# Loading a transformer block's weights behind three semaphores, with the first queries finished beside the first keys

## What is computed

```
x = x + xattn(layernorm(x), ctx)       # q = xn @ Wq + bq; k, v = ctx @ Wk + bk, ctx @ Wv + bv; rope on q and k
x = x + gla(layernorm(x))              # Wq, Wk, Wg1, Wg2, Wv, Wg of its own, scan over 64 tokens, Wo
x = x + ffn(layernorm(x))              # shared expert + 2 of 7 routed experts, hidden width 704
```

## Time and profile before

| | |
|---|---|
| median of 3 runs | 2244.09 us (2237.24 to 2244.69) |
| the profiled execution's own time | 2234.34 us |
| its span in the trace | 2232.5 us |
| busy PE / DVE / ACT / POOL | 1782.9 / 1487.8 / 1097.5 / 748.8 us |
| share of the chain that ended last | PE 43%, DVE 16%, issue 6%, ACT 4%, POOL 3% |

### The profile page before, as it was taken

One profiled execution on the slowest core, in us unless ns is written; L12 is line 12 of the kernel. 1 busy time (PEld: TensorE's weight loads), 2 busy tenths in 40 slices (PEclk: granted clock), 3 DMA queues, 4 the chain that ended last, 5 costly groups with the idle time before them and its releaser, 6 DMA issues.

```text
span 2232.5 us, 51528 instructions
## 1 busy us (share of the span) xinstructions
PE 1782.9 (80%) x19596; PEld 1321.3 (59%) x19596; DVE 1487.8 (67%) x2914; ACT 1097.5 (49%) x2670; POOL 748.8 (34%) x850
## 2 busy tenths in 40 slices
PE   2787787778777877787778777657688999999997
PEld 1454555555555555555555555435567888888886
DVE  1787777877877788788777887746554444444447
ACT  1556555655555556555655565533353333333332
POOL 2333243333333333334333434214501333333320
PEclk8888888989889888888898988868899999999999
DMA  3200010001000100010000000003241111111143
GB/s 84 67 17 17 17 32 17 17 17 32 17 17 17 32 17 17 17 32 17 17 20 29 17 17 19 4 3 107 76 130 43 49 47 44 46 49 46 42 155 125
DMA packets 64092, 88.35 MB, mean 40 GB/s; under 512 B 9488, under 2 KB 52128, under 8 KB 63856
## 3 DMA queue, kind: packets, MB, share of 16 engines
q1 hardware_dynamic: 41232, 36.29, 5.4%
q0 software_dynamic: 10752, 33.17, 4.2%
q10 hardware_dynamic: 11872, 15.60, 2.2%
HBM read 66.68 MB, written 18.35 MB: 38 GB/s over the span
## 4 chain that ended last, share of the span: by engine, by line
PE 43%; DVE 16%; issue 6%; ACT 4%; POOL 3%; ACTq 1%; DMA 0%; DVEq 0%; SPq 0%; POOLq 0%
PE ps L1018 15%; PE ps L709 7%; PE ps L1045 6%; PE ps L717 5%; PE ps L704 5%; POOL experts L654 3%; DVE experts L1447 2%; DVE work L1429 1%; DVE experts L1457 1%; ACT experts L1166 1%; PE ps L1009 1%; PE ps L847 1%; ACT work L1126 1%; DVE experts L1473 1%; DVE x_all L1915 1%
## 5 line engine op out<-in xcount | busy, mean ns | idle before, releaser
L1018 PE MATMUL ps<-work,experts 128*128 128x256 f16 x3564 | 414.7, 278 | 35.3 <-ACT work L1331 22.1
L1018 PEld LDWEIGHTS ps<-work,experts 128*128 (+1 forms) x3564 | 349.3, 100 | 88.5 <-issue 19.8
L704 PE MATMUL ps<-cst,experts 128*128 128x128 f32 x1376 | 238.8, 313 | 122.9 <-DVE experts L1507 56.8
L1126 ACT ACTIVATE experts<-ps 128x512 f16<-128x512 f32 (+3 forms) x416 | 253.2, 646 | 79.8 <-PE ps L704 73.2
L709 PE MATMUL ps<-experts 128*128 128x512 f32 (+1 forms) x640 | 281.6, 581 | 1.4 <-ACT experts L1126 1.4
L704 PEld LDWEIGHTS ps<-cst,experts 128*128 128x128 f32 x1376 | 177.1, 160 | 174.0 <-issue 110.7
L1185 ACT ACTIVATE experts<-ps,experts 128x256 f32<-128x256 f32 x512 | 235.2, 475 | 64.1 <-DVE experts L1447 64.1
L1126 ACT ACTIVATE work<-work 128x768 f16<-128x768 f32 x108 | 90.9, 842 | 338.5 <-PE ps L1050 216.4
L583 POOL TENSOR_TENSOR experts<-experts,cst 128x128 f32<-128x128 f32 x256 | 135.0, 564 | 285.3 <-DVE experts L1457 285.3
L1126 ACT ACTIVATE work<-ps 128x128 f32<-128x128 f32 (+3 forms) x214 | 109.8, 513 | 196.8 <-PE ps L704 195.8
L1045 PE MATMUL ps<-experts,work 128*128 (+1 forms) x1620 | 195.1, 273 | 3.7 <-DVE work L1732 3.7
(11 more groups left out here) (192 smaller groups left out, 3165.8 us busy)
## 6 DMA issues: line engine op xcount, KB each, us to landing
experts<-in_ctx SPq DMA_DIRECT2D x32, 512.0 KB, 4.6
experts<-choice_out POOLq DMA_DIRECT2D x8, 1024.0 KB, 13.5
experts<-in_x SPq DMA_DIRECT2D x32, 128.0 KB, 2.2
token_in<-experts SPq DMA_DIRECT2D x32, 128.0 KB, 1.7
work<-token_in SPq DMA_DIRECT2D x32, 128.0 KB, 2.5
work<-in_L_ffn_routed_gate ACTq DMA_DIRECT2D x8, 352.0 KB, 2.8
work<-in_L_ffn_routed_up ACTq DMA_DIRECT2D x8, 320.0 KB, 3.7
out<-x_all POOLq DMA_DIRECT2D x5, 512.0 KB, 3.3
```

Source lines behind the costliest of these rows:

```text
L704: ins = pe.transpose(bank[:, k * P:(k + 1) * P], a, ident)
L1018: ins = pe.matmul(out, experts_h[:, e, lo:lo + P], e_rows_t[k][:, b * DK + kk, :], start=(kk == 0 and a + b == 0), stop=(kk == DK - 1 and ...
L1126: nc.scalar.activation(dst, src, ACT.Copy).then_inc(done, 1)
```

## The change

The weights' semaphore becomes three. `kv_loaded` counts Wk, Wv and their two biases; `q_loaded` counts Wq and its bias; `weights_loaded` counts the other 26. The first six are issued ahead of pair 1's `load_x`, and the rest come in another order (linear attention's first, the output projection's 16 small ones later). PE and DVE wait for `kv_loaded` just before the first projection and its bias, for `q_loaded` before `project_q` and `q_bias`, and for `weights_loaded` only before the first step. POOL waits for `weights_loaded` only before the first step. Within the start, `project_q` and `turn_q` move ahead of `turn_k` on PE, `q_bias` ahead of `k_add` on DVE, `rope_q` ahead of `split_k` on POOL, and `q_high` and `q_low_turned` ahead of `k_copies` and `v_high` on ACT. No instruction of an engine is added or taken away.

```diff
@@ sync
         load_ctx(Step(0, 0))
         load_x(Step(0, 0))
+        for dst, src in ((w_kv[:, :, 0:D], kmaj(xWk)), (w_kv[:, :, D:2 * D], kmaj(xWv)),
+                         (b_kv[:, 0:D], xbk.partition_broadcast(P)), (b_kv[:, D:2 * D], xbv.partition_broadcast(P))):
+            sp.dma_start(dst, src).then_inc(S["kv_loaded"], 16)
+        for dst, src in ((w_q, kmaj(xWq)), (b_q, xbq.partition_broadcast(P))):
+            sp.dma_start(dst, src).then_inc(S["q_loaded"], 16)
         load_x(Step(0, 1))
...
@@ gpsimd
-        pool.wait_ge(S["weights_loaded"], 16 * WEIGHT_DMAS)
         masks_of(Step(0, 0))
         rope_k(Step(0, 0))
+        rope_q(Step(0, 0))
         split_k(Step(0, 0))
-        rope_q(Step(0, 0))
         split_v(Step(0, 0))
+
+        pool.wait_ge(S["weights_loaded"], 16 * WEIGHT_DMAS)
@@ tensor
         pe.wait_ge(S["consts_loaded"], 16)
-        pe.wait_ge(S["weights_loaded"], 16 * WEIGHT_DMAS)
         pe.wait_ge(S["fill_ready"], 2)
         zero = Step(0, 0)
         turn_ctx(zero)
+        turn_xn(zero)
+        pe.wait_ge(S["kv_loaded"], 64)
         for t in range(4):
             project_kv(zero, t)
-        turn_xn(zero)
-        pe.wait_ge(S["kv_ready"], 4)
-        turn_k(zero)
+        pe.wait_ge(S["q_loaded"], 32)
         project_q(zero)
         pe.wait_ge(S["q_nat_ready"], 1)
         turn_q(zero)
+        pe.wait_ge(S["kv_ready"], 4)
+        turn_k(zero)
+        pe.wait_ge(S["weights_loaded"], 16 * WEIGHT_DMAS)
@@ scalar
         k_high(zero)
+        q_high(zero)
+        q_low_turned(zero)
         k_copies(zero)
         v_high(zero)
-        q_high(zero)
-        q_low_turned(zero)
@@ vector
         dve.wait_ge(S["consts_loaded"], 16)
-        dve.wait_ge(S["weights_loaded"], 16 * WEIGHT_DMAS)
...
         x_norm(zero)
+        dve.wait_ge(S["kv_loaded"], 64)
         for t in range(4):
             kv_bias(zero, t)
         k_cos(zero)
+        dve.wait_ge(S["q_loaded"], 32)
+        q_bias(zero)
         k_add(zero)
-        q_bias(zero)
         q_add(zero)
         q_low(zero)
         q_heads_split(zero)
 
+        dve.wait_ge(S["weights_loaded"], 16 * WEIGHT_DMAS)
         for k, (w, (high, low)) in enumerate(((w_gqk, w_gqk_s), (w_g1, w_g1_s), (w_gvg, w_gvg_s))):
@@
-WEIGHT_DMAS = 3 + 16 + 8 + 5
+WEIGHT_DMAS = 6 + 1 + 16 + 3
```

More of the change, by code:

```diff
@@ L357, in program @@
         cleared mask_step
-        consts_loaded weights_loaded waits_met fill_ready ctx_loaded ctx_turned
+        consts_loaded kv_loaded q_loaded weights_loaded waits_met fill_ready ctx_loaded ctx_turned
         ctx_t_ready kv_done kv_ready k_prod_ready k_swap_ready k_rot_ready k_turned k_t_ready x_stat_ready
@@ L435, in _, with kmaj @@
         load_x(Step(0, 0))
+        def kmaj(w):
+            return w.rearrange("(k p) n -> p k n", p=P)
+        for dst, src in ((w_kv[:, :, 0:D], kmaj(xWk)), (w_kv[:, :, D:2 * D], kmaj(xWv)),
[3 more added lines that the diff above has]
+            sp.dma_start(dst, src).then_inc(S["q_loaded"], 16)
         load_x(Step(0, 1))
         wl = S["weights_loaded"]
-        def kmaj(w):
-            return w.rearrange("(k p) n -> p k n", p=P)
         count = [0]
@@ L446, in wload @@
             count[0] += 1
[L448 to L454, removed]
         wload(w_gqk[:, :, 0:P], kmaj(gWq))
@@ L460, in _ @@
         wload(w_gvg[:, :, D:2 * D], kmaj(gWg))
+        wload(b_o, xbo.partition_broadcast(P))
+        for hp in range(8):
+            for a in range(2):
+                row = (2 * hp + a) * HC
+                wload(w_o[hp * HC:(hp + 1) * HC, a, :], xWo[row:row + HC, :])
         wload(w_go, kmaj(gWo))
         wload(w_r, kmaj(Wr))
[L463 to L466, removed]
         wload(b_g, gbg.partition_broadcast(P))
```

## The result

The changed kernel takes 2217.64 us in the median of 4 runs (2216.41 to 2219.04). The kernel before takes 2244.39 beside it (4 runs, 2237.24 to 2245.24). The ratio is 0.9893, with a 95% interval from 0.9877 to 0.9908: 24 us less by the ratio (20.6 to 27.6), 26.8 by the medians. The forecast was 2221, 22.3 less. The profiled execution took 2217.16, its span is 2215.3, against 2234.34 and 2232.5: only 17.2 less.

What follows compares the result with a forecast made beforehand. The start was bound by waiting for weights not yet needed and by two chains laid end to end, not by an engine. Savings of 16.2 + 0 + 6.1 = 22.3 us from 2244.09 gave 2221.8, stated as 2221; range 2212 to 2230.

Steps and rivals of the forecast that it cites:

- What bounds the start: Before the scores: no engine; some 13 us waiting for weights not yet needed, then two chains laid end to end.
- Part 1: First projection waits only for kv_loaded and starts at 11.1 instead of 27.30: 16.2 us saved (15.2 to 17.4).
- rival (b): Broadcast biases hold kv_loaded, start at 16: 2226.7 at best, 2238 at worst; chance 0.05.
- The bound from below: Earliest first projection by x's path: x lands at 7.3, then 2.63 to the projection, so 9.9.
- Part 2: First projection's start to k_cos: the same 10.1 us as before, nothing saved.
- rival (a): PE runs the whole first projection at half of pair 1's speed, losing 4.9 us: 2226.7; chance 0.12.
- Part 3: From k_cos to the scores: 16.05 us instead of 22.17, 6.1 saved (5.4 to 8.3).
- What costs nothing: Later weights, pair 1's transfers and moved work at the start stay hidden; weights_loaded has ten us of cover.
- A microsecond saved before the scores is one saved at the end: Behind the scores, all 32 steps and the experts wait only for semaphores, so the start's saving passes on.
- Rival (d): The shifted start makes some 28 steps each 1.47 us longer, 41 us lost: 2263; chance 0.03.
- From the profiled execution to the median: Whole time: the median stays 9.75 us above the profiled execution, 2212.0 profiled giving 2221.8.

Runs made afterwards that it cites:

- e1: The changed kernel with its three semaphores and transfer order, but every engine's start in the old order; 2261.6 us beside 2286.01 before, ratio 0.9897.
- e3: The changed kernel with key and value biases on their own semaphore, PE waiting for the two weights only; 2255.49 us, ratio 0.9872 to the kernel before.
- e5: The changed kernel with both the edits of e3 and e4; 2211.98 us beside 2242.54 before, ratio 0.9871.
- e6: The changed kernel delayed by an unneeded first load of Wo's 16 blocks; 2224.31 us beside 2242.54 before, ratio 0.9927.
- e7: e5 plus 12 unread identity transposes in PE's pauses before the first product; 2220.33 us beside 2251.73 before, ratio 0.9874.
- r1: The changed kernel run again, unaltered, on another chip; 2214.05 us beside 2242.54 before, ratio 0.9878.
- e4: The changed kernel with POOL's split_k waiting until DVE's q_low is done; 2255.08 us, ratio 0.9873 to the kernel before.
- r0: The kernel before run again, unaltered, on the chip of r1; 2240.51 us beside 2242.54, ratio 0.9998.
- e8: e7 plus 52 more unread transposes in PE's pause before turn_q; 2219.71 us beside 2251.73 before, ratio 0.9857.
- e2: The changed kernel's new engine order, but one semaphore and the old transfers; 2275.62 us beside 2286.01 before, ratio 0.9945.
- r2: The kernel before, unaltered, one more single profiled execution; 2261.04 us beside 2251.73.

## Why the prediction was right

It forecast the direction and, with 2221 for 2217.6, nearly the time. Step by step:

- **What bounds the start**: right. PE's first transpose came at 5.65, and e1 with the semaphores alone moved the scores by 15.8.
- **Part 1, 16.2 saved**: 15.4. `kv_loaded` was full at 11.9 instead of 11.0, and the near miss is partly luck, since both of its terms were read from counts on a shared semaphore. Wv was to land at 8.45; where the weights have their own semaphore they were there at 9.1 to 10.3. Two broadcasts behind it were to cost 2.55; the biases were there 0.7 to 2.0 after the weights. The two errors pull against each other. e3 showed that the biases do end the wait, so rival (b) is real, in a small size. The bound from below, 9.9 by x's path, was no bound: in the kernel after x landed at 1.71 + 4.4 = 6.1 and not at 7.3, and e5 began at 9.40.
- **Part 2, 0**: 0.8 lost; k_cos came 10.92 behind the first product. Other traces with the new start had 9.28 (e6) to 10.72 (e3), those with the old one 9.35 to 10.46. So rival (a) is real as a mechanism, and nothing shows that the change brings it, since the two spreads overlap. e7 shows where the time goes: 7.8 with PE busy ahead.
- **Part 3, 6.1 saved**: 6.5; the chain was 15.65 (15.64 in r1) where I had 16.05. Two durations were off and cancel in part: k_add ended 6.45 behind k_cos where I had 6.95, because it did not wait for a rope_q instruction but ran beside it (1.51, and rope_q's two 1.95 instead of 1.20). q_low ended 10.15 behind it where I had 10.6. The collision that I argued from one duration (q_add's 2.20) is shown by e4: 0.69 instead of 2.06, 1.35 on the path. The rule of the Trainium skill that I weighed in this part, GPSIMD Engine Reference, section 8, agrees with e4's trace.
- **What costs nothing**: right. SP's queue ran 2.7 later than before at its end (bg issued at 21.20, at 18.53 before), since SP stood up to 1.51 at issues that took 0.47 elsewhere; that stayed inside the cover. bg landed at 21.20 + 4.5 = 25.7, 1.1 later than before, and DVE's weight splits began at 34.97. Pair 1's context was not issued at about 19 before, as I wrote, but at 26.71, since it waits for the first transposes; after, it was issued at 21.78.
- **"A microsecond saved before the scores is one saved at the end"**: right. The stores are 20.6 earlier in the profiled pair and 22.0 in r0 and r1, whose spans differ by 21.9; e6's delay was handed on too. Rival (d) did not come: the 28 stretches from the first to the 29th store took 1250.5 in both kernels.
- **From the profiled execution to the median**: this step failed. I kept the distance of 9.75 between before's profiled execution and its median. After's profiled execution lies 0.5 from its median. The pair of profiled executions shows 17.2, since after's had the longer stretch ahead of the gather. 2221 came within 3.4 of the median all the same. The medians show 26.8, and again 28.5 between r1 and the kernel before beside it.

What stays open: the marks at the scores say 21 to 22.4 saved, the two ratios 20.6 to 27.6 and 22.9 to 31.6. 22.3 lies inside the first and just below the second. Either the runs scatter, or a few us more are saved in the pieces behind. One piece that scatters is the one from the scores to the first store. It took 81.9 to 82.7 in six traces, all at a granted clock of 0.86, and 84.5 to 85.2 in six others at 0.82 or 0.83, and each kind holds kernels with the early start and with the late one (e4 had 83.6 and e8 80.8). e1 and e2 had the longer kind, and so their first stores are only 12.8 and 3.9 ahead of before's. In r2 the 28 middle stretches took 1257.5 where 1250.5 is usual (longer than in any profile of the changed kernel, as its rival had it), and in e2 1253.9, both kernels with the late start; but e8, with the early one, had 1253.7. 14 traces don't settle it.

## What to carry to other kernels

Look first for work that stands idle behind a wait for "all weights", give what is needed first a semaphore of its own, and check in the trace that everything behind that start waits only for its own inputs, so that the saving is passed on. Then look for two chains laid end to end, and interleave them so that the engine with the longest copies gets the last link. Put the saving down to marks in the trace, not to the whole time, where a later stage has a spread as large as what is to be measured. And where transfers share a semaphore, trust only the time at which the last of them has landed.

## What the runs showed of the hardware

- **SP stood longer at some issues of the new order.** It stood 1.51 at the value bias, behind the key bias (0.68 to 1.66 in the nine traces with this order), and 0.90 and 1.36 at the two transfers behind the query bias, against 0.47 for most others. A broadcast ahead is not enough for that: at the tail of the kernel before's queue five of them stood in a row, at 0.43 each. What else it takes was not tested.
- **Broadcasts behind full-size weights.** Both biases were there 6.8 to 7.8 after the second was issued, and 0.7 to 2.0 after the two weights in front of them (e3, e5, e7, e8).
- **A landing on a shared semaphore.** Wv showed 5.3 from issue to landing in the four traces where it shared a semaphore with the biases behind it (after, e1, e4, r1), and 5.9 to 7.1 in the four where it did not.
- **DVE and GpSimd on SBUF.** A 128x512 DVE instruction of two SBUF inputs took 2.06 beside a 2.00 POOL instruction and 0.69 alone (after, e4). Where POOL ran short instructions (rope_q), both sides stretched instead: k_add 1.51 against 1.23, rope_q 1.95 against 1.20.
- **PE's slow first products.** In the kernel after PE ran products 0.86 apart for 6 us at a granted clock of 1.00, and 0.43 apart from 18.03 on; with 12 transposes in the pauses ahead of it the whole took 7.90. The profile's clock column shows only the other fall, to 0.50 in the pause behind. The Trainium skill, TensorE: Matmul & The Clock Gate, Part 1, has the array start at half clock and speed up under sustained activity; the halved spacing agrees with that.
- **The same work, other lengths.** From the first gather to the end 561.3 to 562.2 us in six traces, 570.6 to 575.6 in four of another chip and 598.9 to 608.3 in four of a third, with a granted clock of 0.98 or 0.99 in all of them. PE was busy 541 to 542 us of it in the first case, 548 to 550 in the second and 550 to 555 in the last; what makes up the rest, and whether it is the chip, was not tried.
